# Value products of the first attention in groups of four chunks, with eight probability buffers

## The chip, the cores and the metric

The kernel runs on one core of one Trainium2 chip. The metric is the time of one execution on the device, in microseconds (us). Before the change three runs took 781.73, 784.34 and 785.57 us; their median is 784.34 us.

## The reference

Sixteen images x of 112 rows by 256 and sixteen contexts of 375 rows by 256 go through two blocks. Each block has an attention and a layer of experts, both added to x. The change is in the first attention only:

```python
def _L0_xattn_ref(x, xa, Wqkv, bqkv, Wqkv_aux, bqkv_aux, Wo, bo, g):
    D, H = (256, 16)                       # 16 heads of 16
    qkv = x @ Wqkv + bqkv
    qkv_a = xa @ Wqkv_aux + bqkv_aux
    q, k, v = (_split_heads(c) for c in jnp.split(qkv, 3, axis=-1))
    qa, ka, va = (_split_heads(c) for c in jnp.split(qkv_a, 3, axis=-1))
    p = softmax(q k^T / 4)                 # over the image's 112 rows
    pa = softmax(q ka^T / 4)               # over the context's 375 rows
    out = (p v) * (1 - sigmoid(g)) + (pa va) * sigmoid(g)
    return out @ Wo + bo                   # heads joined again
...
x = x + _L0_xattn_ref(_layernorm(x), ctx_1024, ...)
x = x + _L0_ffn_ref(_layernorm(x), ...)    # 8 experts, each row to the best
x = x + _L1_xattn_ref(ctx_1024, ctx_1024, _layernorm(x), ...)
x = x + _L1_ffn_ref(_layernorm(x), ...)    # 16 experts, with a capacity
```

## The kernel before, in words

The program has four phases with a barrier behind each: `attention0`, `ffn0`, `attention1`, `ffn1`. Everything below is `attention0`.

**Stages and steps.** The phase is written out as 21 steps (`unrolled_steps`), and each engine has its own `step(b)`. In step b, TensorE makes keys, queries and values of image b and of image b - 1, the scores for the row maxima of image b - 2, the attention of image b - 3 and the routing of image b - 4. Steps 3 to 17 have both maxima and attention in them; step 18 has attention and no maxima. The order on each engine is the order in which the step's code is written; engines wait for each other by semaphores.

**The attention of one image** has 16 heads in four groups of four, and 487 keys in four chunks: the image's own 112 rows, and the context's 128, 128 and 119. That makes 16 units, called chunks k = 0 to 15 here: head group k // 4, key chunk k % 4. Each chunk passes three engines:

- Score products (`logits`, line 883): four matmuls on TensorE, one a head, into PSUM bank 4 + k % 2. There are two such banks, so the scores of chunk k wait for the exponential of chunk k - 2.
- Exponential (line 549): one ScalarE instruction, from that bank into a probability buffer, 128 by 448.
- Value products (`values`, line 898): four matmuls with 32 output rows each, which lie beside each other in TensorE's columns, into bank 6 or 7. The records show each as two passes, so a chunk has 8 matmul records.

**The maxima.** For image b - 2, `max_scores` (line 866) makes two products of 96 by 487 a slot, and VectorE takes two reductions of them (lines 755 and 756). The banks are two pairs, so the products of slot k wait for the reductions of slot k - 2. After the eighth slot, four small VectorE instructions (lines 768 to 774) split the maxima into three parts, and TensorE turns them (line 1008).

**The slots.** A step starts with eight slots, called slot 0 to 7 (`pair` in the code). The order on TensorE is:

```python
for pair in range(8):
    logits(b - 3, 2 * pair)
    logits(b - 3, 2 * pair + 1)
    max_scores(b - 2, pair)
    if pair >= 1:
        values(b - 3, 2 * pair - 2)
        values(b - 3, 2 * pair - 1)
values(b - 3, 14)
```

After the slots come the transposes of half of the context (line 947), which wait for the seventh pair of reductions; the transposes for the router (line 1269), which wait for exponential 14; chunk 15 of the values; the transposes of the normed image (line 1001), which wait for the eighth pair of reductions; the other half of the context; the transpose of the maxima (line 1008); the transposes of the value sums (line 840), for which ScalarE first copies banks 6 and 7 (line 554); and the projections of lines 1024 to 1072.

**The probability buffers.** There are four (`probs`), so the exponential of chunk k waits for the values of chunk k - 4 (`pv_done`). In each step all exponentials also wait for all values of the image before.

**Memory.** `early` cuts buffers out of `rings`, an area that holds the weights of the last phase later on. `sb` allocates a buffer by itself.

Of the kernel before, what the change touches and what calls it, by code (L numbers as in the profile page):

```python
# [12 lines left out]
ACT = mybir.ActivationFunctionType  # L13
AX = mybir.AxisListType.X

B, T, D = 16, 112, 256
S = 375
H, DH = 16, 16
# [10 lines left out]
P = 128  # L29
# [199 lines left out]
def attention0(nc, a, g_):  # L229
# [3 lines left out]
    with ExitStack() as phase:  # L233
        def sb(name, shape, dt=F32):
            return g_.sb(name, shape, dt, phase)
# [3 lines left out]
        def early(shape, dt=F32):  # L239

            nonlocal taken
            words = math.prod(shape[1:]) // (1 if dt == F32 else 2)
            view = g_.rings[0:shape[0], taken:taken + words]
            taken += words
            assert taken <= 8 * RING
            if dt != F32:
                view = view.bitcast(dt)
            names = "abcd"[:len(shape) - 1]
            return view.rearrange(f"p ({' '.join(names)}) -> p {' '.join(names)}", **dict(zip(names, shape[1:])))
# [2 lines left out]
        w_aux = early([P, 2, 2 * D])  # L252
        wo = sb("wo", [P, 2, D])
        w_p = early([P, 2, 3, 2, P])
        bias_rows = sb("bias_rows", [3, D])
        bias_turned = sb("bias_turned", [3, 2, P])
        bias_t = sb("bias_t", [P, 2, 3])
        g_wide = sb("g_wide", [P, H])
        inv_gate = sb("inv_gate", [P, 2, H])
# [9 lines left out]
        k_parts = [early([P, 3, 2, KV], BF16) for p in range(2)]  # L269
        q_parts = [sb(f"q_parts{p}", [P, 3, 2, T], BF16) for p in range(2)]  # L270
        k_rest = early([P, 2, KV])
        q_rest = sb("q_rest", [P, 2, T])
        k_stack = [g_.stacks[0:ROWS, p, 0:K_WORDS].bitcast(BF16).rearrange("r (h n) -> r h n", h=H) for p in range(3)]
        q_stack = [g_.stacks[0:ROWS, p, K_WORDS:STACK].bitcast(BF16).rearrange("r (h n) -> r h n", h=H) for p in range(3)]
        k_flat = [k_stack[p].rearrange("r h n -> r (h n)") for p in range(3)]
# [3 lines left out]
        max_rest = sb("max_rest", [T, 2, H])  # L279
        max_parts = sb("max_parts", [T, 2, 3, H], BF16)  # L280
        mt = sb("mt", [QK, T], BF16)
        probs = [sb(f"probs{k}", [P, 4, T]) for k in range(4)]
        pv = [sb(f"pv{u}", [P, 2, 2, T]) for u in range(2)]
        inv_sum = [sb(f"inv_sum{u}", [T, H]) for u in range(2)]
        normed = sb("normed", [T, 2, 2, P // 2])
        mixed_rows = sb("mixed_rows", [T, 2, P])
# [6 lines left out]
        r = router0(nc, g_, phase, bank[4], bank[5])  # L293
# [203 lines left out]
        def _(act):  # L497
# [42 lines left out]
            def step(b):  # L540
                if (b - 3).real():
                    n = b - 3
                    for k in range(16):
                        keys = T if k % 4 == 0 else CHUNKS[k % 4 - 1][1]
                        act.wait_ge(s["logits_mm"], n.count(16, k + 1))

                        act.wait_ge(s["pv_done"], n.count(16, max(k - 3, 0)))
                        src = bank[4 + k % 2][0:keys, 0:4 * T].rearrange("p (j q) -> p j q", j=4)
                        nc.scalar.activation(probs[k % 4][0:keys, :, :], src, ACT.Exp, scale=DH ** -0.5).then_inc(s["exp_done"], 1)  # L549
                    for u in range(2):  # L550
                        act.wait_ge(s["pv_done"], n.count(16, 8 * (u + 1)))
                        if (n - 1).real():
                            act.wait_ge(s["turned_mm"], (n - 1).count(2, u + 1))
                        nc.scalar.copy(pv[u][:, :, :, :].rearrange("p g s t -> p (g s t)"), bank[6 + u][:, 0:4 * T]).then_inc(s["pv_out"], 1)
# [15 lines left out]
                if (b - 2).real():  # L570
                    n = b - 2
# [7 lines left out]
                if (b - 1).real():  # L579
                    n = b - 1  # L580
# [235 lines left out]
        def _(pe):  # L816
# [70 lines left out]
            def values(n, k):  # L887

                g, c = k // 4, k % 4
                pe.wait_ge(s["exp_done"], n.count(16, k + 1))  # L890
                if k in (0, 8) and (n - 1).real():

                    pe.wait_ge(s["mixed_ready"], (n - 1).count(2, k // 8 + 1))
                keys, chunk, o = (T, 3, 0) if c == 0 else (CHUNKS[c - 1][1], c - 1, 1)
                for j in range(4):
                    h = 4 * g + j
                    col = (2 * (g % 2) + o) * T
                    last = nc.tensor.matmul(bank[6 + g // 2][32 * j:32 * j + 32, col:col + T], v[n.parity][0:keys, chunk, h, :],  # L898
                                            probs[k % 4][0:keys, j, :], start=(c <= 1), stop=(c == 0 or c == 3))
                last.then_inc(s["pv_done"], 1)  # L900

            def total(n):
# [54 lines left out]
            def step(b):  # L957
                if (b - 3).real():
                    n = b - 3
# [5 lines left out]
                for pair in range(8):  # L965
                    if (b - 3).real():
                        logits(b - 3, 2 * pair)
                        logits(b - 3, 2 * pair + 1)
                    if (b - 2).real():
                        max_scores(b - 2, pair)  # L970
                    if (b - 3).real():
                        if pair >= 1:
                            values(b - 3, 2 * pair - 2)
                            values(b - 3, 2 * pair - 1)
                if (b - 3).real():
                    values(b - 3, 14)
                if b.c == 2:
                    constant_row()
                if b.real():
# [10 lines left out]
                        pe.wait_ge(s["exp_done"], (b - 3).count(16, 15))  # L990
                    r.turn(pe, b - 4, ident)
                if (b - 3).real():
                    values(b - 3, 15)
                if b.real():
                    pe.wait_ge(s["xn_ready"], b.count(1, 1))
                    if (b - 2).real():
# [7 lines left out]
                if (b - 2).real():  # L1004
                    n = b - 2
# [9 lines left out]
                if (b - 1).real():  # L1015
                    n = b - 1
# [10 lines left out]
                    for h in range(2):  # L1027
                        nc.tensor.matmul(bank[1][0:CHUNKS[2][1], 0:D], ct[n.parity][:, h, 2 * P:S], w_aux[:, h, D:2 * D],
                                         start=(h == 0), stop=(h == 1))
                    for h in range(2):  # L1030
                        last = nc.tensor.matmul(bank[1][0:T, D:2 * D], xt[n.parity][:, h, :], w_x[:, h, 2 * D:3 * D],
                                                start=(h == 0), stop=(h == 1))
# [950 lines left out]
```

## Time and profile before

| What | Value |
|---|---|
| Median of three runs | 784.34 us |
| Span of the profiled execution, first to last instruction | 792.0 us |
| Time of the profiled execution beside its span | none is given |
| Granted TensorE clock over the span | 0.965 |
| TensorE matmul, busy | 724.7 us (91%) |
| TensorE weight load, busy | 568.2 us (72%) |
| VectorE, busy | 418.0 us (53%) |
| ScalarE, busy | 326.5 us (41%) |
| GpSimd, busy | 219.5 us (28%) |
| Steps 3 to 18 of the first attention | from 64.47 us on, the last starts at 415.40 us |

The profile was taken in another execution than the three timed runs, and its span is longer than they are. Matmuls are pipelined and their ends are modelled, so TensorE counts as busy in much of the time that a matmul waits to drain. The starts are the better guide: the distance of two starts is what the first group took, together with what the second waited for. The rows of weight loads also name what ended the time before them.

### The profile page before, as it was taken

To read this page: it belongs to the slowest core of one execution; us is meant where nothing else is said; L and a number is where in the kernel's file an instruction comes from. 1 tells how busy PE (TensorE), PEld (TensorE's weight loads), DVE (VectorE), ACT (ScalarE), POOL (GpSimd) and SP (SyncE) were. 2 spreads that over 40 slices of the span, in tenths; PEclk is the share of its full clock that TensorE was granted. 3 is DMA by queue.
4 is the path that set the end of the run, shared out by engine and by line. 5 is a ranking of instruction groups with operands and counts; after the bars stand their busy time and mean duration, and the time that the engine had idled before them with its cause. 6 is when DMAs were issued, how large, how long until landed. Compare 5 with 4: busy or idle time off the path is not lost. (4 is left out here: it accounts for less than half of the span.)

```text
span 792.0 us, 19429 instructions
## 1 busy us (share of the span) xinstructions
PE 724.7 (91%) x6719; PEld 568.2 (72%) x6720; DVE 418.0 (53%) x1267; ACT 326.5 (41%) x884; POOL 219.5 (28%) x361
## 2 busy tenths in 40 slices
PE   4688999999999999998998699998999988999996
PEld 2445777666677766676665588888788778999995
DVE  2366777787777687774772322222488762111111
ACT  2215655566555566654544133331465551101110
POOL 2402332233332232330312013333355532111111
PEclk9869999999999999999999789999999998999999
DMA  4999977998888998885946549882566642999950
GB/s 154 130 137 118 165 113 120 126 123 134 145 140 146 150 144 118 147 141 81 121 129 191 141 120 246 247 220 63 170 197 205 195 131 60 306 337 335 334 174 16
DMA packets 98984, 128.12 MB, mean 162 GB/s; under 512 B 23363, under 2 KB 83884, under 8 KB 98769
## 3 DMA queue, kind: packets, MB, share of 16 engines
q1 hardware_dynamic: 90625, 115.24, 68.0%
q0 software_dynamic: 3824, 8.46, 4.1%
q10 hardware_dynamic: 4447, 3.30, 1.8%
q8 instruction: 50, 0.82, 0.6%
q14 instruction: 38, 0.30, 0.2%
HBM read 74.68 MB, written 23.88 MB: 124 GB/s over the span
## 5 line engine op out<-in xcount | busy, mean ns | idle before, releaser
L549 ACT ACTIVATE probs<-psum 128x448 f32<-128x448 f32 (+2 forms) x256 | 125.2, 541 | 60.5 <-PE psum L883 59.9
L755 DVE TENSOR_REDUCE neg_max<-psum 112x2 f32<-112x750 f32 x128 | 118.8, 928 | 8.9 <-PE psum L866 7.3
L866 PE MATMUL psum<-stacks 96*128 96x487 bf16 (+1 forms) x256 | 78.3, 389 | 8.6 <-DMA stacks<-q_parts 5.8
L883 PE MATMUL psum<-stacks 102*128 102x112 bf16 (+1 forms) x1024 | 77.5, 215 | 3.6 <-DMA stacks<-mt 2.0
L898 PEld LDWEIGHTS psum<-probs,rings 128*32 128x32 f32 (+2 forms) x2048 | 45.3, 109 | 46.9 <-issue 37.6
L883 PEld LDWEIGHTS psum<-stacks 102*128 102x128 bf16 (+1 forms) x1024 | 54.7, 99 | 33.0 <-ACT probs L549 23.9
L898 PE MATMUL psum<-probs,rings 128*32 128x112 f32 (+2 forms) x2048 | 76.7, 266 | 0.8 <-issue 0.8
L1947 PEld LDWEIGHTS psum<-e_xt,rings 128*128 128x128 f32 x512 | 59.5, 192 | 2.2 <-ACT e_xt L1893 1.3
L1947 PE MATMUL psum<-e_xt,rings 128*128 128x112 f32 x512 | 59.7, 275 | 0.9 <-ACT e_xt L1893 0.9
L1913 DVE SCALAR_TENSOR_TENSOR e_y<-psum,e_x_in 112x256 f32<-112x256 f32 x16 | 7.7, 484 | 98.0 <-PE psum L1961 98.0
L1961 PE MATMUL psum<-rings,e_hid 128*112 128x256 f32 x256 | 57.9, 379 | 1.3 <-DVE e_hid L1920 1.3
L1961 PEld LDWEIGHTS psum<-rings,e_hid 128*112 128x112 f32 x256 | 44.0, 177 | 10.4 <-issue 1.7
L953 PE MATMUL psum<-rings 128*128 128x375 f32 x128 | 48.3, 500 | 1.0 <-issue 1.0
L756 DVE TENSOR_REDUCE neg_max<-psum 112x2 f32<-112x224 f32 x128 | 48.5, 379 | 0.0
L1452 PE MATMUL psum<-t_xt,t_w 128*128 128x128 f32 x336 | 43.9, 287 | 4.8 <-issue 3.4
L1452 PEld LDWEIGHTS psum<-t_xt,t_w 128*128 128x128 f32 x336 | 42.6, 201 | 7.7 <-issue 5.9
L1397 ACT ACTIVATE t_hid<-psum,b 128x128 f32<-128x128 f32 x84 | 26.2, 363 | 52.8 <-PE psum L1452 52.8
L1893 ACT COPY e_xt<-psum 128x224 f32<-128x224 f32 x16 | 5.5, 345 | 100.1 <-PE psum L1932 100.1
L434 POOL TENSOR_TENSOR ln_rstd<-ln_mv,eps 112x1 f32<-112x1 f32 x16 | 3.0, 189 | 149.0 <-DVE ln_mv L629 149.0
L1878 POOL DMA_INDIRECT out<-e_y,e_index x16 | 15.2, 951 | 99.5 <-DMA e_x_in<-sorted 42.3
L1370 POOL DMA_INDIRECT made<-t_y,t_index x21 | 23.8, 1136 | 61.1 <-issue 45.5
L1465 PE MATMUL psum<-stacks,t_hid 128*128 x168 | 39.6, 379 | 0.0
(226 smaller groups left out, 1389.2 us busy)
## 6 DMA issues: line engine op xcount, KB each, us to landing
rings<-in_L_ffn_w SPq DMA_DIRECT2D x32, 1024.0 KB, 7.1
stacks<-rings SPq DMA_DIRECT2D x96, 243.5 KB
ct_dram<-rings SPq DMA_DIRECT2D x16, 375.0 KB, 10.8
a_ct<-ct_dram SPq DMA_DIRECT2D x16, 375.0 KB, 5.1
a_ctx<-in_ctx SPq DMA_DIRECT2D x16, 375.0 KB
stacks<-q_parts SPq DMA_DIRECT2D x96, 56.0 KB
rings<-in_ctx SPq DMA_DIRECT2D x16, 256.0 KB
w<-in_L_ffn_W SPq DMA_DIRECT2D x8, 512.0 KB, 11.5
```

The source lines that it names most:

```text
L549: nc.scalar.activation(probs[k % 4][0:keys, :, :], src, ACT.Exp, scale=DH ** -0.5).then_inc(s["exp_done"], 1)
L755: nc.vector.tensor_reduce(neg_max[:, 0, h:h + 2], psum[0:T, pair:pair + 2, 0:S], AX, ALU.max, negate=True)
L756: nc.vector.tensor_reduce(neg_max[:, 1, h:h + 2], psum[0:T, pair:pair + 2, S:KV], AX, ALU.max, negate=True).then_inc(s["max_done"], 1)
L866: last = nc.tensor.matmul(bank[2 - 2 * (k % 2) + j][0:rows, 0:KV], q_flat[n.third][0:QK, h * T:h * T + rows], k_stack[n.third][0:QK, h, :] ...
L883: last = nc.tensor.matmul(bank[4 + k % 2][0:wide, j * T:(j + 1) * T], k_flat[n.third][:, first:first + wide], q_stack[n.third][:, h, :], s ...
L898: last = nc.tensor.matmul(bank[6 + g // 2][32 * j:32 * j + 32, col:col + T], v[n.parity][0:keys, chunk, h, :], probs[k % 4][0:keys, j, :], ...
L953: last = nc.tensor.matmul(bank[(0, 3)[h]][:, 0:S], w_p[:, a_, 2, h, :], ct[b.parity][:, a_, :], start=(a_ == 0), stop=(a_ == 1))
L1397: nc.scalar.activation(hid[j.parity][:, f, :], up_bank(j, f)[:, f % 2 * P:(f % 2 + 1) * P], ACT.Relu, bias=bias).then_inc(s["hid"], 1)
L1452: last = nc.tensor.matmul(up_bank(j, f)[:, f % 2 * P:(f % 2 + 1) * P], w1_now[j.parity][:, k, f * P:(f + 1) * P], xt2[j.parity][:, k, :], ...
L1465: last = nc.tensor.matmul(bank[6 + n.parity][:, 0:D], hid[n.parity][:, f, :], w2[:, bass.ds(e, 1), f, :].rearrange("p o d -> p (o d)"), st ...
L1947: last = nc.tensor.matmul(bank[2 * e.parity + f // 4][:, f % 4 * C1:(f % 4 + 1) * C1], g.ring1[e.quarter][:, k, f * P:(f + 1) * P], xt[e.p ...
L1961: last = nc.tensor.matmul(bank[6 + n.parity][0:C1, 0:D], hid[n.parity][:, f, :], g.ring2[n.quarter][:, f, :], start=(f == 0), stop=(f == K ...
```

## The change

The order of the value products in a step is changed: slots 2, 4 and 6 have four chunks each, and the last four follow behind the router's transposes. The probability buffers are eight instead of four, and the exponentials wait accordingly. To make room, `q_rest` and two of the new buffers are cut from `rings`, and two small buffers for the bias rows share the memory of the value sums `pv`.

```diff
-        bias_rows = sb("bias_rows", [3, D])
-        bias_turned = sb("bias_turned", [3, 2, P])
...
-        q_rest = sb("q_rest", [P, 2, T])
+        q_rest = early([P, 2, T])
...
-        probs = [sb(f"probs{k}", [P, 4, T]) for k in range(4)]
+        probs = [sb(f"probs{k}", [P, 4, T]) for k in range(6)] + [early([P, 4, T]) for _ in range(2)]
         pv = [sb(f"pv{u}", [P, 2, 2, T]) for u in range(2)]
+        bias_rows, bias_turned = [u[0:3, :, :, :].rearrange("r g o t -> r (g o t)")[:, 0:D] for u in pv]
+        bias_turned = bias_turned.rearrange("r (a n) -> r a n", a=2)
...
-                        act.wait_ge(s["pv_done"], n.count(16, max(k - 3, 0)))
+                        act.wait_ge(s["pv_done"], n.count(16, max(k - 7, 0)))
                         src = bank[4 + k % 2][0:keys, 0:4 * T].rearrange("p (j q) -> p j q", j=4)
-                        nc.scalar.activation(probs[k % 4][0:keys, :, :], src, ACT.Exp, scale=DH ** -0.5).then_inc(s["exp_done"], 1)
+                        nc.scalar.activation(probs[k % 8][0:keys, :, :], src, ACT.Exp, scale=DH ** -0.5).then_inc(s["exp_done"], 1)
...
-                                            probs[k % 4][0:keys, j, :], start=(c <= 1), stop=(c == 0 or c == 3))
+                                            probs[k % 8][0:keys, j, :], start=(c <= 1), stop=(c == 0 or c == 3))
...
                     if (b - 2).real():
                         max_scores(b - 2, pair)
                     if (b - 3).real():
-                        if pair >= 1:
-                            values(b - 3, 2 * pair - 2)
-                            values(b - 3, 2 * pair - 1)
-                if (b - 3).real():
-                    values(b - 3, 14)
+                        if pair in (2, 4, 6):
+                            for k in range(4):
+                                values(b - 3, 2 * pair - 4 + k)
...
                     r.turn(pe, b - 4, ident)
                 if (b - 3).real():
-                    values(b - 3, 15)
+                    for k in range(12, 16):
+                        values(b - 3, k)
```

## Rows read from the trace of the kernel before

**Rows 1.** Windows: us, busy of each engine (instructions), clock, DMA share, GB/s

```profile
160.51:183.89 23.38, 23.32 (x280) 16.51 (x279) 18.04 (x51) 13.95 (x34) 7.21 (x10) 1.00 0.89 142
...
301.50:324.89 23.39, 23.33 (x281) 16.52 (x280) 18.06 (x51) 13.94 (x34) 7.22 (x10) 1.00 0.90 142
```

**Rows 2.** Costliest groups of the page: busy, mean ns, idle before and its releaser

```profile
L549 ACT ACTIVATE probs<-psum 128x448 f32<-128x448 f32 (+2 forms) x256 | 125.2, 541 | 60.5 <-PE psum L883 59.9
```

**Rows 3.** Timeline of TensorE's matmuls in one step: start us, us, line, operation

```profile
160.51 0.66 PE L883 MATMUL psum<-stacks 102*128 102x112 bf16 x8
...
162.15 0.58 PE L866 MATMUL psum<-stacks 96*128 96x487 bf16 x2
162.66 0.59 PE L898 MATMUL psum<-probs,rings 112*32 112x112 f32 x16
163.19 0.57 PE L883 MATMUL psum<-stacks 102*128 102x112 bf16 x8
163.59 0.58 PE L866 MATMUL psum<-stacks 96*128 96x487 bf16 x2
164.10 0.59 PE L898 MATMUL psum<-probs,rings 128*32 128x112 f32 x16
164.62 0.57 PE L883 MATMUL psum<-stacks 102*128 102x112 bf16 x8
...
170.79 0.58 PE L866 MATMUL psum<-stacks 96*128 96x487 bf16 x2
171.30 0.78 PE L898 MATMUL psum<-probs,rings 112*32 112x112 f32 x24
172.01 0.54 PE L947 MATMUL psum<-ident,rings 128*128 128x128 f32 x3
...
172.68 0.40 PE L898 MATMUL psum<-probs,rings 119*32 119x112 f32 x8
173.01 0.41 PE L1001 MATMUL psum<-ident,xn 112*128 112x112 f32 x2
...
173.58 0.25 PE L1008 MATMUL psum<-ident,max_parts 112*96 112x112 bf16 x1
```

**Rows 4.** Timeline of TensorE's weight loads, slot 1 of the same step

```profile
161.50 0.21 PEld L883 LDWEIGHTS psum<-stacks 102*128 102x128 bf16 x4 [0.39 <-ACT probs L549]
161.94 0.21 PEld L883 LDWEIGHTS psum<-stacks 102*128 102x128 bf16 x4 [0.22 <-ACT probs L549]
```

**Rows 5.** Timeline of ScalarE, slots 0 to 2 of the same step

```profile
160.91 1.99 ACT L549 ACTIVATE probs<-psum 112x448 f32<-112x448 f32 x4 [0.48 <-PE psum L883]
163.59 0.98 ACT L549 ACTIVATE probs<-psum 112x448 f32<-112x448 f32 x2 [0.70 <-PE psum L883]
```

**Rows 6.** Timeline of VectorE in the same step: ends of reductions, last maxima part

```profile
162.77 0.37 DVE L756 TENSOR_REDUCE neg_max<-psum 112x2 f32<-112x224 f32 x1
...
165.69 0.38 DVE L756 TENSOR_REDUCE neg_max<-psum 112x2 f32<-112x224 f32 x1
...
173.33 0.19 DVE L774 TENSOR_TENSOR max_parts<-max_rest,max_parts 112x32 bf16<-112x32 f32 x1
```

**Rows 7.** Timeline of the last step with attention, step 18

```profile
415.40 0.56 PE L883 MATMUL psum<-stacks 102*128 102x112 bf16 x8
...
416.83 0.21 PEld L883 LDWEIGHTS psum<-stacks 102*128 102x128 bf16 x4 [0.22 <-ACT probs L549]
...
424.65 0.41 PE L1269 MATMUL psum<-ident,r_rows 112*128 112x112 f32 x2
...
425.32 1.37 PE L840 MATMUL psum<-ident,pv 128*112 128x128 f32 x8
```

**Rows 8.** Line 743 by destination: duration ns min/median/max, first and last start

```profile
L743 DVE SCALAR_TENSOR_TENSOR rings<-psum,bias_t,rings x32: 323/330/338, 19.9 to 375.7; 128x112 f32<-128x112 f32 x32
L743 DVE SCALAR_TENSOR_TENSOR q_rest<-psum,bias_t,q_parts x32: 323/324/326, 20.2 to 376.0; 128x112 f32<-128x112 f32 x32
```

**Rows 9.** Timeline of a later step: a stall of TensorE

```profile
364.99 0.32 PE L840 MATMUL psum<-ident,pv 128*112 128x128 f32 x1 [2.63 <-issue]
```

## The prediction

> **What bounds the kernel now.** I read the busy shares by window first, since the change touches one phase only, the first attention. Four whole steps of it take 23.38 to 23.39 us each, with TensorE at 1.00 of its clock and its matmuls busy for 23.32 or 23.33 of it [rows 1]. The step length repeats, so TensorE's order of work sets the pace here. Busy time of pipelined matmuls says little about what holds them, so next comes the group list: ScalarE's exponentials (0.541 us each, 256 of them) sit idle for 60.5 us in all, 59.9 of it behind the score products [rows 2]. At this point ScalarE looks like an engine with room. Last the timelines of one step, engine by engine, counted from its first score product (t = 0 is 160.51): these decide.
>
> In a slot with value products TensorE takes 0.40 us for eight score products, 0.51 for two max products and 0.52 for the value products of two chunks, then the next slot begins: 163.19, 163.59, 164.10, 164.62, about 1.44 a slot [rows 3]. Three chunks take 0.71 (171.30 to 172.01) and one takes 0.33 (172.68 to 173.01) [rows 3]. The three sizes lie on one line: 0.14 fixed for a group plus 0.19 per chunk.
>
> Slot 0 of each step has no value products, and it shows what such a slot does. Its score products start at 0, but those of slot 1 start at 0.99 (161.50) and, for the second bank, at 1.43 (161.94), both behind an exponential; the max products of slot 1 follow at 1.64 and the values at 2.15 [rows 3, 4]. The exponentials explain these figures: the first starts 0.40 after the score products do, two take 0.98, four in a row 1.99 [rows 5]. With 0.54 for one, the second starts 0.44 behind the first; they end at 0.94 and 1.38, and TensorE goes on 0.05 later. With only two score banks, a chunk's scores can't start until the exponential of two chunks earlier has read its bank. In a 1.44 slot that time passes under the value products. In a slot without them it is bare.
>
> **The change part by part.**
>
> *Order of the value products.* Slots 1, 3, 5 and 7 lose theirs; slots 2, 4 and 6 get four chunks, and the last four chunks come after the step's first transposes. No instruction is added or removed on any engine; what moves is TensorE's queue alone. A value group of four isn't in the trace. Low end: 0.71, a fourth chunk for nothing; high end: 1.04, two groups of two. I take 0.90 from the line through the rows for one, two and three chunks (0.71 + 0.19).
>
> A light slot and the heavy slot behind it, by slots 0 and 1: scores of the heavy slot at 0.99, second bank 1.43, max products 1.64, values 1.64 + 0.51 = 2.15, and the next light slot at 2.15 + 0.90 = 3.05. Two slots now take 2.88. So each such pair costs 0.17 more, although it saves a group's fixed 0.14: the score products of the heavy slot wait instead.
>
> Now a step. Slots 0 and 1 as today, max products of slot 1 at 1.64. Slot 2: third and fourth exponential run from 1.39 and 1.83 to 1.93 and 2.37, so its second bank starts at 2.42 and its max products could at 2.63. They also need the first reduction, which ends at 162.77 + 0.37, that is 2.63, plus 0.06 to reach TensorE: 2.69 [rows 6]. Values 3.20, slot 3 at 4.10 (today 4.11). Slot 5 at 7.15, slot 7 at 10.20, its max products 0.41 later at 10.61; today these start at 170.79, which is 10.28. So the last max products come 0.33 later.
>
> What follows them: two reductions, four small VectorE instructions, and the transpose of the row maxima, whose weights load 2.79 after those max products (173.58), 0.06 after the last of the four ends (173.33 + 0.19) [rows 3, 6]. TensorE's own path from there in the new order is 0.51 for the max products, 0.67 for the transposes (172.01 to 172.68), 0.90 for the four chunks and 0.57 from 173.01 to 173.58: 2.65, which stays under the 2.79. So the values moved behind the transposes are hidden, with 0.14 to spare, and the maxima set the step: +0.33. The rest of the step is TensorE's string as before, 280 matmul records in 23.38 us [rows 1], and shifts whole. The last chunk ends at 12.69 against 12.50 today [rows 3], 0.19 later where everything behind the maxima is 0.33 later, so the copy of the value sums that waits for it gains room.
>
> Steps with both score and max products: 15, so 15 x 0.33 = 4.95 us.
>
> *The last step* has score products but no max products (its first at 415.40) and is paced by the exponentials even now: the second bank of slot 1 waits until 416.83, 1.43 after the start [rows 7]. By the same recurrence, values start 0.30 behind the second bank (0.21, and the 0.10 that a change from full to narrow tiles adds): slot 2 at 1.99 and 2.43, values 2.73 to 3.63; each further pair 0.99 + 0.44 + 0.30 + 0.90 = 2.63, so slot 5 at 6.26 and slot 7 at 8.89. The routing transpose waits for its first exponential, 0.99 later, 9.88, and takes about 0.34; the four last chunks end at 11.12. Today the transposes of the value sums start at 425.32, 9.92 [rows 7]. So +1.2 us. They feed the last image's router and the sort that the next phase starts from, so I count it whole; if it were covered it would be 0.
>
> *Eight probability buffers.* Exponentials wait for values seven chunks back instead of three. In the new order exponential 8 needs the values of slot 2 and exponential 12 those of slot 4, both over a slot earlier, so nothing waits. It gains nothing by itself either, because today's releaser of the exponentials is the score products [rows 2]: the limit is the score banks, and there are still two.
>
> *Memory moved*: q_rest and two probability buffers into the shared ring area, the bias rows into the value-sum buffers. The same instruction takes 324 ns into q_rest and 330 ns into the ring area [rows 8]: between 0 and 32 x 6 ns = 0.2 us, on VectorE beside TensorE's string. The bias rows are used once, long before the first value sums. I take 0.
>
> Sum: 4.95 + 1.2 = 6.2 us. The profiled execution has a span of 792.0 us, and no time of its own is given beside it; it becomes 798.2. The runs without the profiler have a median of 784.34, 7.7 below the span; a stall like the 2.63 us for which the trace shows no releaser [rows 9] is part of that. The difference goes onto the median: 784.34 + 6.2 = 790.5 us.
>
> **A rule against this.** The fixed 0.14 us of a value group [rows 3] is weighed here. The Trainium skill, "TensorEngine Tiling (Array Packing)", Key Properties, says that changing the tiling mode, not just the tile, drains TensorE. The trace agrees that there is a price per group. By that rule alone, eight value groups a step become four, 4 x 0.14 x 16 = 9.0 us are saved, and the time is 775.3; by the exponentials' rows it is 790.5. The rule counts no wait of the score products.
>
> **The rivals.**
> *The drains decide (faster).* If the score products weren't held in the new light slots, TensorE's string alone would count: slots 0 and 1 1.00 + 0.91, three heavy slots 1.81 each, slots 3 and 5 0.91 each, 0.41 in slot 7: last max products at 9.6, 0.68 earlier, 15 x 0.68 = 10 us, 774 us. For it: the fixed 0.14, and that two exponentials take 0.98 where the pair of slots has 2.7 in all. Against it: the two waits in every slot 1 [rows 4] and in the last step [rows 7]. Chance 0.08.
> *The step absorbs it (same).* If something outside TensorE's string holds the later part of the step, a later slot 7 costs nothing there, and only the last step's 1.2 remains: 785.5. For it: the stall of [rows 9]. Against it: four steps equal to 0.01 us [rows 1]. Chance 0.17.
> *VectorE falls behind too (slower).* Reductions come in bunches. Slot 4's max products, at 5.74, need the third reduction, which runs behind the router's statistics and ends today at 165.69 + 0.38, 5.56, so 5.62 for TensorE [rows 6]: 0.12 to spare. From a delay of over 0.12 on, each 0.1 us costs 1.5 us over 15 steps; if the third reduction came half of one (0.45) later, 15 x 0.33 = 5 more, 795.5. Against it: nothing in the new order delays that reduction. Chance 0.10.
>
> **How the numbers follow.** Forecast 0.65, by itself 788.4 to 793. With a value group at 0.71, slot 7 comes 0.57 earlier: 15 x (0.33 - 0.57) + 1.2 - 0.76 = -3.2, 781.2; with 1.04, 15 x 0.75 + 1.2 + 0.56 = 13.0, 797.3. Three sizes on a line make both ends unlikely, so the range is 783 to 796; it leaves out the faster rival and the far ends. A difference of 0.5% (3.9 us) is about what a measurement of this kernel can tell. Faster 0.08, slower 0.65 + 0.10 = 0.75, same 0.17.
>
> **What would show it.** Steps of 23.7 us. In the timeline of TensorE: value groups of 32 records lasting 0.90 until the next slot; slots 3, 5 and 7 at 4.10, 7.15 and 10.20; in slots 2, 4 and 6 weight loads of score products released by an exponential, twice. The transpose of the maxima at 13.40 and still released by VectorE. In the last step the transposes of the value sums at 11.1. Steps shorter than 23.38 would refute the wait; steps of 23.7 with a total unchanged would mean that the end of the phase absorbs it; heavy slots without such waits would refute the recurrence.

## The result, and the profile after

The changed kernel takes 794.1 us (median of 4 runs, 793.26 to 796.95), the kernel before 784.96 us (4 runs, 781.73 to 787.0). The ratio is 1.0112, with a 95% interval of 1.0073 to 1.0151: 5.7 to 11.9 us slower. The forecast was 790.5 us, the range 783 to 796. The profiled execution of the changed kernel took 793.52 us with a span of 791.6 us.

The first view is again the busy shares of two undisturbed steps (us, busy of the engines with their instructions, granted clock, DMA share, GB/s). They answer to [rows 1].

```profile
112.42:136.19 23.77, 23.43 (x280) 16.78 (x279) 18.06 (x51) 13.96 (x34) 7.39 (x10) 1.00 0.79 118
231.83:255.60 23.77, 23.43 (x283) 16.79 (x281) 18.04 (x50) 13.95 (x34) 7.09 (x10) 1.00 0.89 140
```

A step is 23.77 us where it was 23.38 or 23.39 [rows 1], with the same instructions, the same busy time on VectorE and ScalarE and the clock at 1.00: 0.39 more, and all of it is waiting. Next the costliest groups of the page. The exponentials stand there as two groups now, since two of the eight buffers are cut from `rings`; they answer to [rows 2].

```profile
L549 ACT ACTIVATE probs<-psum 112x448 f32<-112x448 f32 (+1 forms) x192 | 94.0, 541 | 32.2 <-PE psum L883 29.7
...
L549 ACT ACTIVATE rings<-psum 128x448 f32<-128x448 f32 x64 | 31.3, 541 | 33.8 <-PE psum L883 33.8
```

An exponential still takes 541 ns. Idle before them are 32.2 + 33.8 = 66.0 us against 60.5 [rows 2]: ScalarE waits more for TensorE, not less. The timeline of TensorE's matmuls in the step that starts at 112.42 answers to [rows 3] (start us, us, line, operation).

```profile
112.42 0.66 PE L883 MATMUL psum<-stacks 102*128 102x112 bf16 x8
...
113.42 0.81 PE L883 MATMUL psum<-stacks 102*128 102x112 bf16 x8
114.06 0.58 PE L866 MATMUL psum<-stacks 96*128 96x487 bf16 x2
114.48 0.75 PE L883 MATMUL psum<-stacks 102*128 102x112 bf16 x8
115.11 0.59 PE L866 MATMUL psum<-stacks 96*128 96x487 bf16 x2
115.63 0.98 PE L898 MATMUL psum<-probs,rings 112*32 112x112 f32 x32
116.54 0.57 PE L883 MATMUL psum<-stacks 102*128 102x112 bf16 x8
...
118.19 0.58 PE L866 MATMUL psum<-stacks 96*128 96x487 bf16 x2
...
119.61 0.57 PE L883 MATMUL psum<-stacks 102*128 102x112 bf16 x8
...
122.68 0.57 PE L883 MATMUL psum<-stacks 102*128 102x112 bf16 x8
123.08 0.58 PE L866 MATMUL psum<-stacks 96*128 96x487 bf16 x2
...
125.88 0.25 PE L1007 MATMUL psum<-ident,max_parts 112*96 112x112 bf16 x1
```

Counted from 112.42: slot 1 at 1.00, slot 2 at 2.06, the first value group at 3.21, slot 3 at 4.12, the max products of slot 4 at 5.77, slot 5 at 7.19, slot 7 at 10.26, the last max products at 10.66, the transpose of the maxima at 13.46. The value group of 32 records takes 116.54 - 115.63 = 0.91. The weight loads of the heavy slots 2, 4 and 6 show what their score products waited for.

```profile
114.42 0.26 PEld L883 LDWEIGHTS psum<-stacks 102*128 102x128 bf16 x4 [0.26 <-ACT probs L549]
114.85 0.21 PEld L883 LDWEIGHTS psum<-stacks 102*128 102x128 bf16 x4 [0.18 <-ACT probs L549]
...
117.54 0.21 PEld L883 LDWEIGHTS psum<-stacks 102*128 102x128 bf16 x4 [0.50 <-issue]
117.98 0.21 PEld L883 LDWEIGHTS psum<-stacks 102*128 102x128 bf16 x4 [0.22 <-ACT rings L549]
...
120.61 0.24 PEld L883 LDWEIGHTS psum<-stacks 102*128 102x128 bf16 x4 [0.50 <-ACT probs L549]
121.05 0.21 PEld L883 LDWEIGHTS psum<-stacks 102*128 102x128 bf16 x4 [0.19 <-ACT probs L549]
```

Each heavy slot has two waits, the second about 0.44 behind the first, like slot 1 of before [rows 4]. One of the six bears no name; it is the same wait, since the exponential that it needs is the first of the two in this row of ScalarE. It starts at 116.95 and so ends at 117.49, 0.05 ahead of the load.

```profile
116.95 0.98 ACT L549 ACTIVATE rings<-psum 128x448 f32<-128x448 f32 x2 [1.09 <-PE psum L883]
```

The last step with attention, by TensorE's matmuls, answers to [rows 7].

```profile
421.83 0.56 PE L883 MATMUL psum<-stacks 102*128 102x112 bf16 x8
...
431.79 0.41 PE L1268 MATMUL psum<-ident,r_rows 112*128 112x112 f32 x2 [0.44 <-ACT rings L549]
...
433.03 1.37 PE L840 MATMUL psum<-ident,pv 128*112 128x128 f32 x8
```

The transposes of the value sums start at 11.20 instead of 9.92 [rows 7].

**Where the time is.** The profiled execution of before was a long one of its kind: from step 18 to its end it took 376.6 us, where a second profile has 370.3. So the two kernels were run once more on one chip, with a profile each; their spans are 781.8 and 791.9 us. Read from the starts of the steps in TensorE's timeline:

| Stretch | old order again | new order again | difference |
|---|---|---|---|
| to the first score product of step 3 | 62.46 | 64.04 | 1.58 |
| steps 3 to 17 | 349.09 | 356.43 | 7.34 |
| step 18 to the first tile of `ffn0` | 37.63 | 38.69 | 1.06 |
| from there to the end | 332.62 | 332.74 | 0.12 |

The first row isn't the change's: the other runs with the old order start step 3 at 63.83 to 64.47, those with the new one at 63.10 to 64.75. In the second row 0.39 a step shows in the clean steps (0.33 in steps 3 and 17), which makes 13 x 0.39 + 2 x 0.33 = 5.7. The other 1.6 stands in four disturbed steps. The lengths of steps 4 to 15 are:

```
old 23.38 23.39 24.52 23.38 23.39 23.38 23.39 24.07 23.38 23.38 23.39 27.95
new 23.72 23.77 24.73 25.61 23.79 23.77 23.78 24.79 23.78 23.77 23.78 27.99
```

What exceeds the clean step sums to 6.44 in the old order and 8.04 in the new one (7.96 in the first profile of the changed kernel). Step 7 has 1.84 of it, and nothing in the old order. This excess is a second quantity to follow through the experiments, since the prediction had none.

### The profile page after: what moved, and what is told of

The parts are those of the page before. It is cut to its first block and busy times, and to the rows that moved or that the text cites. A ratio compares the mean times of both kernels' runs of the same rounds, so it can differ in the third digit from the quotient of the medians.

```text
span 791.6 us, 19429 instructions
## 1 busy us (share of the span) xinstructions
PE 719.1 (91%) x6719; PEld 569.7 (72%) x6720; DVE 418.2 (53%) x1267; ACT 326.4 (41%) x884; POOL 219.4 (28%) x361
## 5 line engine op out<-in xcount | busy, mean ns | idle before, releaser
L549 ACT ACTIVATE probs<-psum 112x448 f32<-112x448 f32 (+1 forms) x192 | 94.0, 541 | 32.2 <-PE psum L883 29.7
L883 PE MATMUL psum<-stacks 102*128 102x112 bf16 (+1 forms) x1024 | 84.8, 214 | 7.5 <-DVE c_wide L811 1.9
L898 PE MATMUL psum<-probs,rings 128*32 128x112 f32 (+2 forms) x1536 | 50.5, 263 | 1.3 <-issue 1.3
L898 PEld LDWEIGHTS psum<-probs,rings 128*32 128x32 f32 (+2 forms) x1536 | 34.9, 109 | 22.3 <-ACT probs L549 18.3
L1451 PE MATMUL psum<-t_xt,t_w 128*128 128x128 f32 x336 | 41.3, 276 | 4.6 <-issue 3.7
L1451 PEld LDWEIGHTS psum<-t_xt,t_w 128*128 128x128 f32 x336 | 40.4, 192 | 6.8 <-issue 4.8
L549 ACT ACTIVATE rings<-psum 128x448 f32<-128x448 f32 x64 | 31.3, 541 | 33.8 <-PE psum L883 33.8
## 6 DMA issues: line engine op xcount, KB each, us to landing
ct_dram<-rings SPq DMA_DIRECT2D x16, 375.0 KB, 10.5
```

The lines of the kernel that those rows point to most:

```text
L549: nc.scalar.activation(probs[k % 8][0:keys, :, :], src, ACT.Exp, scale=DH ** -0.5).then_inc(s["exp_done"], 1)
L883: last = nc.tensor.matmul(bank[4 + k % 2][0:wide, j * T:(j + 1) * T], k_flat[n.third][:, first:first + wide], q_stack[n.third][:, h, :], s ...
L1451: last = nc.tensor.matmul(up_bank(j, f)[:, f % 2 * P:(f % 2 + 1) * P], w1_now[j.parity][:, k, f * P:(f + 1) * P], xt2[j.parity][:, k, :], ...
```

## The experiments

**1. Exponentials halved, in either order.** The theory is that the score products of heavy slots wait for exponentials; the rival was that they wait for something else and the step is longer for another reason. An exponential of half the columns takes that wait away and leaves TensorE's work as it is. These kernels leave out the exponentials of two heads in each group of four.

```diff
-  nc.scalar.activation(probs[k % 8][0:keys, :, :], src, ACT.Exp, ...)
+  nc.scalar.activation(probs[k % 8][0:keys, 0:2, :], src[:, 0:2, :], ACT.Exp, ...)
...
-  probs[k % 8][0:keys, j, :], start=...
+  probs[k % 8][0:keys, j % 2, :], start=...
```

Old order:

> The old order of the value products, with exponentials over two of a group's four heads (the values of the other two read the first two's, so the output is not the reference's). An exponential should take about 0.35 us instead of 0.54. Theory (the score products wait for the exponentials wherever a slot has no value products): the waits in slot 1 go, the last max products start at about 9.94 us of the step instead of 10.28, a step takes about 23.05 us instead of 23.38. Rival (the waits in slot 1 are a cost of the step's start): slot 1 and the step stay as they are.

New order:

> The new order (four chunks of values in slots 2, 4, 6 and behind the transposes), with the same halved exponentials. Theory: the waits of the score products in slots 1, 2, 4 and 6 go; what is left are the reductions, which the max products of slots 2 and 4 wait for (2.69 and 5.62 us); last max products at about 10.07 us, a step about 23.2 us: 0.13 longer than the old order with halved exponentials, where the whole exponentials make it 0.39 longer. Rival one (the groups of four or the moved buffers cost by themselves): the step stays 0.39 longer than the old order's. Rival two (the exponentials are all of it): the step is 0.5 us shorter than the old order's, by four drains of 0.14.

Measured: old order 779.81 us, ratio 0.9934 (0.9904 to 0.9964), clean step 23.38; new order 787.99 us, 1.004 (1.001 to 1.007), clean step 23.32. The new order's 0.39 is gone, and 0.06 more. But the old order's step did not get shorter, which was a miss (forecast 23.05); its 5.1 us less stand in the excess of steps 4 to 15, which is 1.62 instead of 6.44. TensorE's timeline in slot 1 of the old order with halved exponentials says why.

```profile
159.34 0.57 PE L866 MATMUL psum<-stacks 96*128 96x487 bf16 x2 [0.16 <-DVE xs L800]
```

From the start of its step, 157.70, this is again 1.64: VectorE's line 800, the addition to x of an earlier image, which the max products of slot 1 also wait for, ends there as late as the exponentials did. Two things held slot 1, and the forecast had named one. In the new order with halved exponentials another row takes over, behind the last slot.

```profile
259.86 0.59 PE L866 MATMUL psum<-stacks 96*128 96x487 bf16 x2
...
264.39 0.58 PE L866 MATMUL psum<-stacks 96*128 96x487 bf16 x2
265.13 0.54 PE L947 MATMUL psum<-ident,rings 128*128 128x128 f32 x3 [0.16 <-DVE neg_max L756]
```

Its last max products are at 10.15 (step start 254.24; forecast 10.07), and the transposes behind them wait for VectorE's reductions.

**2. Reductions cut too.** If exponentials and reductions both cover the saving of longer value groups, it must come out when both are short. These kernels leave out, besides, all but 112 of the context's 375 columns in one of the two reductions.

```diff
-  nc.vector.tensor_reduce(neg_max[:, 0, h:h + 2], psum[0:T, pair:pair + 2, 0:S], AX, ALU.max, negate=True)
+  nc.vector.tensor_reduce(neg_max[:, 0, h:h + 2], psum[0:T, pair:pair + 2, 0:T], AX, ALU.max, negate=True)
```

Old order:

> The old order with halved exponentials, and the larger reduction over 112 of the context's 375 keys (so the output is not the reference's); a pair of reductions should take about 0.65 us instead of 1.2. Theory: TensorE's own string is left, last max products at about 9.94 us, the transpose of the maxima at about 12.7, a step about 23.05 us, as with halved exponentials alone.

New order:

> The new order with halved exponentials and the smaller reductions. Theory: with both waits gone the drains are all that differs: last max products at about 9.5 us, the transpose of the maxima at about 12.15, a step 0.58 us shorter than the old order's with the same halves (about 22.45), some 9 us less in all. Rival (groups of four or the moved buffers cost by themselves): still about 0.39 us a step longer than the old order.

Measured: old order 777.5 us, 0.9886 (0.983 to 0.9942), clean step 23.35; new order 776.81 us, 0.9876 (0.9812 to 0.994), clean step 22.45. One clean step of the new order by windows, and its timeline:

```profile
326.05:348.50 22.45, 22.30 (x281) 17.02 (x279) 13.94 (x51) 11.02 (x34) 7.09 (x10) 1.00 0.92 147
```

```profile
326.05 0.66 PE L883 MATMUL psum<-stacks 102*128 102x112 bf16 x8
...
330.32 0.58 PE L866 MATMUL psum<-stacks 96*128 96x487 bf16 x2
330.74 0.61 PE L883 MATMUL psum<-stacks 102*128 102x112 bf16 x8
331.19 0.58 PE L866 MATMUL psum<-stacks 96*128 96x487 bf16 x2
331.70 0.59 PE L898 MATMUL psum<-probs,rings 112*32 112x112 f32 x16
...
335.71 0.58 PE L866 MATMUL psum<-stacks 96*128 96x487 bf16 x2
...
338.22 0.21 PE L1007 MATMUL psum<-ident,max_parts 112*96 112x112 bf16 x1
```

The last max products come at 9.66 and the transpose of the maxima at 12.17 (forecast 9.5 and 12.15), and the grouped order is 0.90 a step shorter than the old one, where 0.58 was forecast. The old order's step missed its forecast of 23.05 again; slot 1 is still held by line 800, as this row of the step that starts at 157.11 shows.

```profile
158.74 0.58 PE L866 MATMUL psum<-stacks 96*128 96x487 bf16 x2 [0.15 <-DVE xs L800]
```

So the saving of longer groups is real; in the true kernel the exponentials and the reductions stand in its way. It is larger than the fixed 0.14 of a group [rows 3], because part of the price stands ahead of the group: two max products take 0.42 when score products follow (330.32 to 330.74) and 0.51 when value products do (331.19 to 331.70). Four groups fewer make an estimated 4 x (0.14 + 0.09) = 0.92.

Yet some 12 us a run should follow: 0.90 in each of steps 4 to 15, 0.60 each in steps 16 and 17, and 0.22 in step 3. The two times differ by 0.7. The excess of steps 4 to 15 is 1.90 in the old order and 15.81 in the new one: 13.9 given back. With halved exponentials alone it is 1.62 and 11.82, and steps 3 to 17 together take 343.68 and 352.34; these 8.7 answer to the 8.2 us between the times.

**3. The parts of the change.** Both kernels again, the buffers and the moved memory with the old order, and the new order with step 18 in the old one.

```diff
 # buffers alone: eight buffers, moved memory, and
+  if pair >= 1:
+      values(b - 3, 2 * pair - 2)
+      values(b - 3, 2 * pair - 1)
...
 # step 18 in the old order: groups of four only where
+  if (b - 3).real() and (b - 2).real():
```

The old order again:

> The kernel before, unchanged, profiled a second time. Theory: steps of 23.38 us again, last step of the attention starting at 415 us, give or take a few us of stalls; its span comes out nearer to the timed median (some 783 us) than the first profile's 792.0, whose phases behind the attention were long. Rival (the profile of before was typical): a span of about 792 again.

The new order again:

> The changed kernel, unchanged, timed in more rounds. By its own trace 15 steps are 0.38 us longer and the last step 1.28 us: 7.0 us, a ratio of 1.009. If the time is more than 9 us longer (1.0115), something outside the steps costs too.

The buffers alone:

> Eight buffers and the moved memory, with the old order of the value products. Theory: nothing, steps of 23.38 us, a time within 0.3% of the kernel before. Rival (the buffers in the shared ring area or the shared bias rows cost): part of the 9 us is here, a ratio of 1.003 or more, and steps longer than 23.38.

The last step in the old order:

> The new order everywhere but in the last step, the one without max products, which keeps the old order. Theory: that step's transposes of the value sums come at 9.92 us instead of 11.20, and all that follows up to the end of the phase comes 1.28 us earlier, counted from the step's start. Rival (the end of the phase covers it): the transposes come earlier, the last scatter of rows and the end of the phase do not.

Measured: 785.34 us, 1.0023 (0.9994 to 1.0051), for the old order; 797.27, 1.0187 (1.0152 to 1.0221), for the new one; 785.98, 1.0013 (0.9988 to 1.0037), for the buffers; 792.51, 1.0117 (1.0073 to 1.0161), with the old last step. Buffers and moved memory cost nothing, and a clean step with them is 23.39. The last step by TensorE's timeline:

```profile
419.25 0.56 PE L883 MATMUL psum<-stacks 102*128 102x112 bf16 x8
...
429.17 1.37 PE L840 MATMUL psum<-ident,pv 128*112 128x128 f32 x8
```

That is 9.92 again, so the 1.28 belong to the groups in step 18. The span falls by 3.3: 1.4 of it up to the next phase, and 1.7 in step 15 (26.30 against 27.99), where the clock differs (experiment 5). The second time of the new order, 797.27, is 3.2 above its first; its runs went from 793.86 to 802.64. By the sign that was named before this run (a ratio over 1.0115), something outside the clean steps costs too.

**4. Shorter steps.** If the wait of a light slot's successor is the cost, an order that keeps groups of four without light slots must give the step back: two groups of scores around the max products of two slots, then four values. The second kernel also moves VectorE's router statistics from slot 1 to slot 3.

```diff
+  for pair in (2, 4, 6):
+      for k in range(2): logits(n, 2 * pair + k)
+      for k in range(2): max_scores(b - 2, pair + k)
+      for k in range(2, 4): logits(n, 2 * pair + k)
+      for k in range(4): values(n, 2 * pair - 2 + k)
...
-                        if k == 1:
+                        if k == 3:
                             r.stats(dve, b - 4, xs, s["x1_ready"])
```

The order alone:

> Another order in which no score products lie bare. Slots 0 and 1 as before the change, with two chunks of values in slot 1; then three rounds of: scores of two chunks, the max products of two slots, scores of two chunks, values of four chunks; the last two chunks behind the transposes; the last step in the old order. Theory: the two max products cover the exponentials, no score products wait for them behind slot 1; the second max products of the first two rounds wait for a reduction instead (3.83 and 6.76 us of the step), last max products at 9.40, transpose of the maxima at about 12.95, a step 0.1 us shorter than the old order's: 1 to 2 us less in all. Rival (groups of four cost by themselves): steps longer than 23.4.

With the statistics moved:

> The same order in rounds, with the router's statistics on VectorE behind the fourth pair of reductions instead of the second. Theory: the reduction that the second round waits for comes earlier, last max products at about 9.2, transpose of the maxima at about 12.8, a step 0.3 us shorter than the old order's: some 4 us less in all, 0.5%. Rival: the statistics only move, and a step is as with the rounds alone.

Measured: 792.93 us, 1.0105 (1.0059 to 1.0151), clean step 23.28; and 795.21 (six runs, 792.6 to 804.64; 794.5 without the longest), 1.0137 (1.0097 to 1.0176), clean step 23.02. A clean step of the first kernel, by windows:

```profile
217.24:240.52 23.28, 22.93 (x280) 17.05 (x279) 18.03 (x51) 13.94 (x34) 7.22 (x10) 1.00 0.89 143
```

Both steps came about as forecast, 0.1 and 0.36 shorter than in the old order, so light slots, and not groups of four by themselves, made the steps longer. The forecasts of the times, 1 to 2 and 4 us below the old order, were misses: neither kernel is faster than it. In the first, a clean step gains 0.49 on the changed kernel, but step 3 takes 29.67 instead of 24.30, behind a stop of 4.41 us, and the excess of steps 4 to 15 is 8.98 instead of 7.96. Steps 3 to 17 together take 356.63 against 357.42, and the times differ by 1.2. No order tried beat the kernel before.

**5. The stretches without a releaser.** Most of the excess is stops of TensorE that the trace puts down to "issue". Three weight loads after such stops, from the changed kernel's first profile:

```profile
153.29 0.61 PEld L1027 LDWEIGHTS psum<-rings 128*119 128x119 f32 x3 [0.89 <-issue]
175.33 0.15 PEld L898 LDWEIGHTS psum<-rings 119*32 119x32 f32 x5 [2.02 <-issue]
...
370.76 2.09 PEld L1023 LDWEIGHTS psum<-rings 128*128 128x128 f32 x8 [2.52 <-issue]
```

In its second profile the same stop in step 7 is 2.03 us, at the same instruction. The old order has none there; its stops are in steps 6, 11 and 15, where the new order has some too. Step 15 has a second part. Its windows in the old order, from the second profile and from the kernel with the buffers alone, are:

```profile
344.39:372.34 27.95, 25.26 (x281) 17.68 (x279) 16.91 (x48) 13.97 (x34) 6.49 (x8) 0.94 0.68 91
```

```profile
346.21:372.36 26.15, 23.58 (x281) 16.53 (x280) 16.90 (x48) 13.95 (x34) 6.49 (x8) 1.00 0.73 97
```

The stops in them are alike, 2.86 and 2.74 us, but the granted clock is 0.94 in one and 1.00 in the other, and the step 1.8 us shorter. The kernel with the old last step has 1.00 there too. By these two kernels the excess of steps 4 to 15 is 4.6 in the old order and 6.3 in the new one, so 1.7 remain between the orders.

The theory for the stops: they hang on the place in TensorE's instruction stream. The rival: on what the step is doing. A kernel with sixteen idle matmuls more ahead of the first step, 64 records, tells them apart.

```diff
             pe.wait_ge(s["consts"], 6)
+            g_.keep_busy(bank[3], 16)
```

> The changed kernel with 16 more matmuls on TensorE at the program's start (64 more instructions in its stream), where it waits for the first loads anyway. The changed kernel has a stall of 2.0 us with no releaser in the trace in step 7, in chunk 15 of the values, in every profile; the old order has none there. Theory (TensorE's instructions arrive in portions counted from the program's start, and the dense group of four chunks runs dry at the end of one): the stall leaves that place; a step of its own length 23.77 stands there. Rival (the step's data or transfers cause it): the stall stays in chunk 15 of step 7 with 2.0 us.

Measured: 796.18 us, 1.0162 (1.012 to 1.0205), clean step 23.76, excess 8.58. The stops have moved to steps 5, 10 and 14, and step 7 is clean. One of them:

```profile
247.33 0.50 PEld L948 LDWEIGHTS psum<-ident,rings 128*128 128x128 f32 x3 [3.99 <-issue]
```

Last, whether the weight loads of the first expert layer, issued one a step from step 6 to 13, lie in the way.

```diff
-                if FIRST <= b.c < FIRST + E0:
-                    load_expert(b - FIRST)
+                if 14 <= b.c < 18:
+                    for e in range(2):
+                        load_expert(Item(0, 2 * (b.c - 14) + e, B))
```

> The new order with one change: the eight 512 KB loads of the first expert layer's weights are issued two a step in steps 14 to 17 instead of one a step in steps 6 to 13. Theory (the stretches in which TensorE waits for nothing that the trace names are portions of its instructions that come late, because they queue behind such transfers; in the second run of the new order the load of step 7 was issued 3.7 us before the 2.0 us stretch in chunk 15 of the values): that stretch shrinks from 2.03 us to under 1, those of steps 6 and 11 (0.9 and 1.3) shrink too, the sum over steps 6 to 13 of what exceeds the clean step of 23.77 falls from 3.9 to under 2 us; the clean step itself stays 23.77. Rival (these transfers don't matter; the place in the instruction stream alone decides): 2.0 us remain in step 7 and 3.9 in the sum. The whole time may lie higher, up to 3 us, if the weights are then late for the experts, so only steps 6 to 13 are compared.

Measured: 799.76 us, 1.0179 (1.015 to 1.0208), clean step 23.77. The theory of this run fell. The weight loads after the stops of steps 7 and 11:

```profile
174.20 0.15 PEld L899 LDWEIGHTS psum<-rings 119*32 119x32 f32 x5 [2.02 <-issue]
...
274.61 0.18 PEld L948 LDWEIGHTS psum<-ident,rings 119*128 119x128 f32 x1 [3.24 <-issue]
```

2.02 us remain in step 7, and step 11 stops for 3.24 us instead of 1.33. The excess of steps 6 to 13 is 10.2, not under 2. Windows of that kernel, for the stretches from each stop to its step's end, and of the stop in step 7 itself, show a second price:

```profile
172.43:174.20 1.77, 0.00 (x0) 0.00 (x0) 0.65 (x4) 0.00 (x0) 0.00 (x0) 1.00 1.15 109
174.20:187.03 12.83, 12.83 (x72) 10.75 (x72) 5.76 (x20) 5.79 (x17) 1.43 (x3) 0.87 0.37 80
...
274.61:287.92 13.31, 13.31 (x62) 10.91 (x63) 5.76 (x20) 5.01 (x15) 1.43 (x3) 0.78 0.20 60
```

Behind the stops the granted clock falls to 0.87 and 0.78 for the rest of the step, part of it at the lower of the two levels. In the second profile of the new order the clock stays at 1.00 behind the same 2.03 us stop, and step 7 costs 1.84; here it costs 3.48. The window there, from the stop to the step's end:

```profile
173.91:185.08 11.17, 11.17 (x72) 9.23 (x72) 5.66 (x20) 5.71 (x17) 1.43 (x3) 1.00 0.55 138
```

In step 11 of the kernel with the late loads, 5.81 us are lost for a stop of 3.24.

## Why the prediction was right, and where its sizes were off

**The light slots.** Confirmed row by row. Slots 3, 5 and 7 were forecast at 4.10, 7.15 and 10.20 and came at 4.12, 7.19 and 10.26; the value group 0.90 and came at 0.91; a pair of slots 3.05 and came at 3.07. The last max products slip by 0.38 instead of 0.33: three pairs, 0.02 each. The exponential is the releaser in the heavy slots, and with shorter exponentials the cost goes (experiment 1). The recurrence from slots 0 and 1 of before was enough to see it.

**The maxima.** Forecast 13.40, found 13.46, and VectorE's last small instruction is still what ends before it:

```profile
125.63 0.19 DVE L774 TENSOR_TENSOR max_parts<-max_rest,max_parts 112x32 bf16<-112x32 f32 x1
```

It ends at 125.82, 0.06 ahead of the transpose, as in [rows 6]. The values behind the first transposes are hidden.

**The last step.** Forecast 1.2, found 1.28, and undone by its old order. That it counts whole is near the mark too: the stretch from step 18 to the next phase's first tile is 1.06 longer than in the old order, and 1.41 longer than with the old last step alone.

**Buffers and memory.** Forecast 0, found a ratio of 1.0013 with 1 inside its interval.

**The sum.** By steps it is now 5.7 + 1.28 = 7.0, where the forecast had 4.95 + 1.2 = 6.2. The terms that were there are 0.8 too small. Missing altogether is the term for stops without a releaser, 1.5 in the changed kernel's first profile (7.96 - 6.44) and 1.7 in the pair of kernels with the clock at 1.00 in step 15; most of it is the new stop of step 7. Together 8.5 to 8.7, against 9.1 measured, in an interval of 5.7 to 11.9. The step that failed is a sentence of the sum: "a stall like the 2.63 us for which the trace shows no releaser is part of that", by which the difference between span and median went over unchanged. By the weight loads that stall is 2.86 us, and the old order run again has it at the same 2.86 in a span of 781.8, so it was no part of the difference; and such stalls don't stay when the order on TensorE changes.

**The rivals.** "The drains decide" was wrong as a forecast, but its saving exists: 0.90 a step once exponentials and reductions are short, more than the 0.56 of four groups' fixed 0.14 [rows 3], which left out the 0.09 ahead of each group. The Trainium skill, "TensorEngine Tiling (Array Packing)", Key Properties, says that a change of tiling mode drains TensorE; experiment 2 agrees that fewer changes can pay. The saving was there and it wasn't the bound. "The step absorbs it" was refuted: every clean step is longer. "VectorE falls behind" did not decide: the max products of slot 4 follow their own score products at 5.77, forecast 5.74. With halved exponentials they come at 5.62 (259.86 in a step that starts at 254.24), the very figure of that rival for the third reduction.

**What stays open.** Why the second series of the new order had a longer median (797.27) than the first (794.1), while their profiles have excesses of 8.04 and 7.96, was not settled. The granted clock over the span was 0.973 in the shortest run of the second series (793.86) and 0.964 in the longest (802.64), an estimated 7.4 us more of lost clock (800.9 x 0.036 against 791.9 x 0.027), so the clock is likely part of it. Only the shortest run has a profile. The interval of that series (1.0152 to 1.0221, 11.9 to 17.3 us) lies above the 8.5 to 8.7 us that the traces account for.

## What to carry to other kernels

Before work is gathered into longer groups, look for the slots that lose it and ask what time it was covering there: a slot of the present kernel that already has none is the model for it. Then follow two quantities through the experiments, the length of a clean step and the sum of what exceeds it, because among the kernels that compute the reference's result those with the shortest steps were not the fastest. A wait that is taken away often leaves a second one at nearly the same time: slot 1 was held by the exponentials and by VectorE's line 800 alike.

## What the runs showed of the hardware that was not expected

**Instruction portions.** The page of the second profile of the new order lists a queue of kind "instruction" (packets, MB, share):

```profile
q8 instruction: 49, 0.80, 0.5%
```

Its DMA view from 71.30 to 407.50 us shows 31 such packets, and the busy view of that stretch TensorE's records.

```profile
q8 instruction: 31, 0.51, 0.9%
```

```profile
71.30:407.50 336.20, 324.03 (x3841) 231.54 (x3840) 245.46 (x675) 191.72 (x465) 94.36 (x132) 0.99 0.86 134
```

A packet is 0.80 / 49 = 0.0163 MB, and one comes for each (3841 + 3840) / 31 = 248 matmul and weight load records. No other engine has nearly so many instructions. So these look like TensorE's own. The Trainium skill, "Advanced Engine Details and Errata", ISA Cache, states lines of 16 KB or 256 instructions; the size agrees, and 248 records are near that count.

Read in windows of 0.1 us, the start of such a packet lies ahead of the end of each stop of over 1 us that was compared, in either order:

| Kernel | stop ends (length) | packet starts | between |
|---|---|---|---|
| old order again | 149.02 (1.18) | 145.3 | 3.7 |
| old order again | 361.20 (2.86) | 357.4 | 3.8 |
| new order again | 173.91 (2.03) | 170.2 | 3.7 |
| new order again | 270.77 (1.33) | 267.8 | 3.0 |
| new order again | 369.39 (2.52) | 365.5 | 3.9 |
| 64 records more | 127.41 (1.02) | 123.6 | 3.8 |
| 64 records more | 247.33 (3.99) | 243.7 | 3.6 |
| shorter steps | 80.44 (4.41) | 76.9 | 3.5 |
| shorter steps | 159.75 (3.74) | 156.5 | 3.3 |
| loads late | 174.20 (2.02) | 170.5 | 3.7 |
| loads late | 274.61 (3.24) | 270.6 | 4.0 |

TensorE goes on 3.0 to 4.0 us after a packet starts, whether it has stopped for 1.0 us or for 4.4. It is the late packets that have a stop behind them: in the second profiles of the two orders, from step 4 to step 15, just five packets start over 14 us after the one before (18.6 and 16.5 us in the old order, 16.7, 14.6 and 16.7 in the new one), and they are the five of the table. That, and the move of the stops with 64 records more, fits an engine that has run out of instructions until the next portion is there. It would also tell why groups of 64 records in 0.91 us are a bad neighbour: at that pace a portion of 248 would last 3.5 us, where a step of some 560 records in 23.77 us uses one in 10.5. The dense groups as the reason for more stops are argued, not shown: no kernel changed the density alone, and the old order was not run with its stream shifted. Nor is it shown why a portion is at times asked for so late: before the packet at 170.2 there was none for 16.7 us, and the weight loads taken away from there changed nothing.

**The clock behind a stop.** Stops of 2.02 and 3.24 us were followed by a granted clock of 0.87 and 0.78 to the step's end, and a stop of 2.03 us in another run of the same order by 1.00. The old order has both prices in step 15: 0.94 over the step behind a stop of 2.86 us, 1.00 behind one of 2.74. So a stop of one length has two prices, which may be part of why the times spread.
